# Attention scores from 32-row strips of TensorE, queries unpadded, on one core

## The reference, cut to what matters

```
x = x + conv51x51(groupnorm(x))                   # depthwise
t = tokens(x)
t = t + attn1(ln(t))   # masked: local | every 16th | first 4 keys, and a key counts only if its spike flag is set
t = t + ffn(ln(t))     # up to 33 steps; each may attend (no mask), then apply a hidden layer of 128
# attention of a sample b:  softmax(Q K^T / sqrt(32)) V, 256 x 256 scores, 32 wide
# spike flag of a key: a sequential leaky sum over the 256 tokens has crossed 1.0 in some sample
```

## Time and profile before

| what | value |
|---|---|
| median of 3 runs | 198.55 us (194.80, 198.55, 198.94) |
| profiled execution, its own time | 194.72 us |
| its span, first to last instruction | 192.6 us |
| mean granted TensorE clock | 0.965 of full |
| busy: PE, DVE, ACT, POOL | 163.9, 134.2, 106.5, 63.5 us |
| static attention from its first row maximum | 58.5 us on |
| loop attentions | about 105.7 to 138 and 146.5 to 179 us |

### The profile page before, as it was taken

One profiled execution on the slowest core, in us unless ns is written; L12 is line 12 of the kernel. 1 busy time (PEld: TensorE's weight loads), 2 busy tenths in 40 slices (PEclk: granted clock), 3 DMA queues, 4 the chain that ended last, 5 costly groups with the idle time before them and its releaser, 6 DMA issues.

```text
span 192.6 us, 4240 instructions
## 1 busy us (share of the span) xinstructions
PE 163.9 (85%) x1255; PEld 111.2 (58%) x1256; DVE 134.2 (70%) x382; ACT 106.5 (55%) x319; POOL 63.5 (33%) x153
## 2 busy tenths in 40 slices
PE   7999997773898998888966899998676999997970
PEld 5779754331684765656523687775334977673420
DVE  1363668839948889896554789789475897987371
ACT  3464511429768656565552687665375685664350
POOL 8850000100073455453600036555300075546000
PEclk9999999997599999999999999999999999999696
DMA  5900000000000000000001000000000000000003
GB/s 146 334 12 0 3 0 3 0 3 2 0 2 0 2 0 3 0 0 19 2 0 21 0 0 2 3 0 0 3 17 0 0 0 0 0 0 0 0 0 114
DMA packets 3020, 3.33 MB, mean 17 GB/s; under 512 B 889, under 2 KB 2361, under 8 KB 3002
## 3 DMA queue, kind: packets, MB, share of 16 engines
q1 hardware_dynamic: 2858, 2.85, 4.8%
q10 hardware_dynamic: 144, 0.25, 0.4%
HBM read 2.58 MB, written 0.53 MB: 16 GB/s over the span
## 4 chain that ended last, share of the span: by engine, by line
PE 61%; DVE 16%; ACT 8%; issue 7%; POOL 2%; DMA 2%; DVEq 1%; SPq 1%; POOLq 0%; ACTq 0%
PE bank L555 17%; PE bank L528 8%; PE bank L615 6%; PE bank L542 5%; ACT qz L989 4%; PE bank L798 3%; PE bank L679 3%; PE bank L512 3%; DVE big L1285 3%; PE bank L633 3%; PE bank L600 2%; POOL prob L448 2%; DMA wa<-wa_dram 2%; ACT prob L913 1%; ACT qz L1093 1%
## 5 line engine op out<-in xcount | busy, mean ns | idle before, releaser
L448 POOL TENSOR_SCALAR prob<-prob,einv 128x256 f32<-128x256 f32 x96 | 44.7, 478 | 58.9 <-DVE einv L1280 58.7
L1285 DVE COPY big<-bank 128x512 f32<-128x512 f32 x48 | 32.9, 685 | 5.8 <-PE bank L528 5.7
L913 ACT ACTIVATE prob<-bank,nmax 128x256 f32<-128x256 f32 x64 | 29.8, 474 | 11.6 <-DVE nmax L1272 11.6
L528 PE MATMUL bank<-ident,prob 128*128 128x128 f32 x192 | 30.2, 280 | 6.5 <-POOL prob L448 6.4
L555 PE MATMUL bank<-hT,qz 128*128 128x256 f32 x128 | 32.7, 383 | 0.0
L528 PEld LDWEIGHTS bank<-ident,prob 128*128 128x128 f32 x192 | 21.4, 140 | 18.2 <-POOL prob L448 14.1
L1272 DVE TENSOR_REDUCE nmax<-bank 128x2 f32<-128x512 f32 x32 | 21.6, 686 | 4.8 <-PE bank L555 4.6
L555 PEld LDWEIGHTS bank<-hT,qz 128*128 128x128 f32 x128 | 22.3, 190 | 3.6 <-issue 1.6
L913 ACT ACTIVATE prob<-minus,nmax 128x256 f32<-128x256 f32 x32 | 16.0, 500 | 8.9 <-DVE nmax L1269 7.9
L555 PE MATMUL bank<-kt,qz 128*128 128x256 f32 x64 | 16.6, 387 | 0.9 <-ACT prob L913 0.9
L913 ACT ACTIVATION_READ_ACCUMULATOR prob<-bank,nmax 128x1 f32 x64 | 13.0, 203 | 0.0
(11 more groups left out here) (172 smaller groups left out, 246.3 us busy)
## 6 DMA issues: line engine op xcount, KB each, us to landing
xrev<-xrev_dram SPq DMA_DIRECT2D x1, 512.0 KB, 4.6
xin<-xtok_dram SPq DMA_DIRECT2D x1, 512.0 KB, 5.6
out_dram<-outT SPq DMA_DIRECT2D x2, 256.0 KB, 3.3
maskc<-maskc_dram SPq DMA_DIRECT2D x1, 256.0 KB, 5.5
kx<-kx_dram ACTq DMA_DIRECT2D x1, 248.0 KB, 3.1
wx<-wx_dram SPq DMA_DIRECT2D x1, 216.0 KB, 3.6
constf<-constf_dram SPq DMA_DIRECT2D x1, 186.0 KB, 4.7
wa<-wa_dram SPq DMA_DIRECT2D x3, 56.0 KB, 1.8
```

The source lines that it names most:

```text
L448: last = nc.gpsimd.tensor_scalar(prob[b % NPB][:, ih, :], prob[b % NPB][:, ih, :], einv[:, b, ih:ih + 1], 1.0, ALU.mult, ALU.mult)
L528: mm = pe.transpose(bank[2 + b % 2][:, jh * S + ih * P:jh * S + (ih + 1) * P], prob[b % NPB][:, ih, jh * P:(jh + 1) * P], ident)
L913: e = nc.scalar.activation(prob[b % NPB][:, ih, :], scores, ACT.Exp, bias=nmax[:, b, ih:ih + 1], scale=-1.0 if masked else 1.0, accum_out= ...
L1285: nc.vector.tensor_copy(flat(probT[b % NTB]), bank[2 + b % 2][:, :]).then_inc(s_PT, 1)
```

## The change

- qz becomes qT (128, 4, 256), unpadded, and the fill of qz with zeros goes.
- `scores` takes a list of samples. Each product uses only the sample's 32 rows of queries and keys, at the row strip 32 q of TensorE (`tile_position=(q * C, 0)`), and the strips are issued next to each other: first four samples, then two at a time, after `turn_pe(b)` of an even b and ahead of `weigh_pe`. There are four score banks, SCORES = (0, 1, 4, 5), and a fourth `minus` buffer.
- Reuse of a score bank waits in the masked attention for the row maximum, no longer for the exponentials.
- The ring of tasks has two banks. Query, key and value projections work on two groups at once: half as many tasks, of 512 columns, each drained by one copy of 128 x 512.
- DVE stays three samples ahead with its row maxima.
- The filler products between the first masked scores and the first turn are 20 ahead of the spike wait and 10 behind the transposes, instead of 6 behind them; 5 more follow in both kernels.

```
-        RING = 3
-        SCORES = (0, 1, 4)
+        RING = 2
+        SCORES = (0, 1, 4, 5)
...
-        PRE = "A" + "A" + "AD" + "A" + "AAAA" + "AAAA" + "AAAA" + "D" + "AA"
+        PRE = "A" + "A" + "AD" + "A" + "AA" + "AA" + "AA" + "D" + "AA"
-        LPRE = "ADAD" + "ADAD"
+        LPRE = "AD" + "AD"
...
-            nc.gpsimd.memset(qz[:, :, :], 0.0).then_inc(s_zero, 1)
...
-            def scores(b):
-                if b >= AHEAD:
-                    wait(pe, s_P, base, b - AHEAD + 1)
-                if not masked and b % GB == 0:
-                    t.drained(pe, b // GB + 1)
-                for ih in range(NH):
-                    mm = pe.matmul(bank[SCORES[b % AHEAD]][:, ih * S:(ih + 1) * S], qz[:, b, ih * P:(ih + 1) * P],
-                                   keys[:, b // GB, :], start=True, stop=True)
-                mm.then_inc(s_S, 1)
-            for b in range(AHEAD):
-                scores(b)
+            def scores(batches):
+                last = batches[-1]
+                if last >= AHEAD:
+                    wait(pe, s_nm if masked else s_P, base, last - AHEAD + 1)
+                if not masked and batches[0] % (2 * GB) == 0:
+                    t.drained(pe, batches[0] // (2 * GB) + 1)
+                for ih in range(NH):
+                    for b in batches:
+                        g, q = divmod(b, GB)
+                        rows = slice(q * C, (q + 1) * C)
+                        mm = pe.matmul(bank[SCORES[b % AHEAD]][:, ih * S:(ih + 1) * S], qT[rows, g, ih * P:(ih + 1) * P],
+                                       keys[rows, g, :], start=True, stop=True, tile_position=(q * C, 0))
+                        if ih == NH - 1:
+                            mm.then_inc(s_S, 1)
+            scores(range(AHEAD))
             if meanwhile:
                 meanwhile()
             if masked:
+                masked(bank[2], 20)
                 pe.wait_ge(s_spk, 1)
                 product_pe(pe, st, K_CNT, onesb[:, :], spk[:, :], S)
                 for h in range(NH):
                     transposed_pe(pe, K_RES + h, tok, h)
-                masked(bank[2], 6)
+                masked(bank[2], 10)
             for b in range(MAIN):
-                if b + AHEAD < B:
-                    scores(b + AHEAD)
                 if masked and b == 0:
                     masked(bank[2], 5)
                 turn_pe(pe, base, b)
+                if b % 2 == 0 and b + AHEAD < B:
+                    scores(range(b + AHEAD, b + AHEAD + 2))
...
-                    for g in range(0, NG, 2):
-                        t.filled(act, g)
-                        for q in range(GB):
-                            rows = slice(q * C, (q + 1) * C)
-                            cp = nc.scalar.activation(qz[rows, g * GB + q, :], t.bank(g)[rows, 0:S], ACT.Copy)
-                        cp.then_inc(s_da, 1)
+                    t.filled(act, 0)
+                    nc.scalar.activation(flat(qT[:, 0:2, :]), t.bank(0)[:, :], ACT.Copy).then_inc(s_da, 1)
...
-                for b in range(AHEAD):
+                for b in range(AHEAD - 1):
                     row_max(base, b, masked)
...
-                    if b + AHEAD < B:
-                        row_max(base, b + AHEAD, masked)
+                    if b + AHEAD - 1 < B:
+                        row_max(base, b + AHEAD - 1, masked)
```

More of the change, by code:

```diff
@@ L466, in _ @@
             for g in range(NG):
-                wait(pool, s_da, 0, count("A", STATIC[:K_V + g + 1]))
+                wait(pool, s_da, 0, count("A", STATIC[:K_V + g // 2 + 1]))
                 for h in range(NH):
@@ L674, in _, with values @@
             to_tokens(3)
-            def values(t, k, src, g, w):
+            def values(t, k, src, i, w):
                 t.fill_wait(pe, k)
                 for h in range(NH):
-                    mm = pe.matmul(t.bank(k)[:, h * P:(h + 1) * P], src[:, g, h * P:(h + 1) * P], w, start=True, stop=True)
+                    for g in (2 * i, 2 * i + 1):
+                        at = (2 * h + g % 2) * P
+                        mm = pe.matmul(t.bank(k)[:, at:at + P], src[:, g, h * P:(h + 1) * P], w, start=True, stop=True)
                 mm.then_inc(s_task, 1)
@@ L915, in attention_act @@
                 e.then_inc(s_P, 1)
[L916 to L917 removed]
+                if meanwhile and b == 0:
+                    meanwhile()
                 if not masked and b >= 6 and (b - 6) % GB == 0:
```

83 lines of the change are left out of this document (37 added, 46 removed).

## The result

The changed kernel took 199.59 us (median of four executions, 198.95 to 201.56), the kernel before on the same chip 196.68 us (194.3 to 198.94). The ratio is 1.0255, with a 95% interval of 1.0213 to 1.0297: slower by 2.6%, where 1.6% faster was forecast.

What follows compares the result with a forecast made beforehand. PE was taken as the bound (busy 19.50 of 20.00 us), DVE close behind (17.66). Loops 2.4 + static 1.3 - clock 0.45 = 3.2 us gained: 198.55 - 3.2 = 195.3 us, -1.6%; range for 8 in 10, 190.5 to 198.8.

Steps and rivals of the forecast that it cites:

- The clock: Static front: PE idle 3.0 us before the spikes may drop to 1.2 GHz; cost 0 to 0.9, taken as 0.45 us.
- the last way to be wrong: Closing sign against the forecast: clock low in one of the attentions themselves, where PE has more idle time; no size given.
- Rival 2: Static front: clock stays at 1.2 GHz through all 15 fillers, turn 0 comes 3 us late; total 197.6 us; chance 20%.
- Rivals 1 and 3: 1: DVE's rate bounds, groups 5.4, 188.9 us, 15%; 3: strips don't overlap or shape changes cost more, 205 us, 10%.
- Rival 4: Attention start: the first scores at once could still wait for the second projection bank; left at nothing.
- The pair of scores: PE in the attentions: two samples in row strips take 1.00 us instead of 1.74; same for the first four.
- The loop attention's steady part: Loop groups of four samples stay at about 6.7 us, DVE's copy stalling 1.1 behind scores and weigh; no gain.
- the 0.2 that they were to give back: Loop attentions: small weight copies (four of 0.22, one of 0.18) fall into DVE's stall, returning 0.2 us.
- The forecast's sum for before: Loop attention before the change: PE's own work for four samples, shape changes included, put at 6.5 to 6.6 us.
- The loop attention's start: Each loop attention: merged projections, fewer query copies and four samples' scores at once bring turn 0 1.2 us earlier.
- The static attention: Earlier count and first row maximum (57.4), shorter periods (7.15 per four samples): 1.3 us gained at full clock.
- The wait for `K_RES + 1`: Static attention: second half of `tok` waits for K_CNT's drain, ACT's copy runs 58.25 to 58.9, taking back most of 1.1 us.

Runs made afterwards that it cites:

- fill_all: Changed kernel plus POOL's value bias after the spikes, 32 spare products ahead of them, two before turns, eight behind each loop attention's values: 190.16 us, ratio 0.9796; repeat 190.41.
- bias_late: Changed kernel, but POOL adds the value bias only after the spikes are ready: 203.35 us (198.07 to 205.84).
- front_held: Changed kernel with POOL's bias after the spikes and 32 instead of 20 spare products ahead of them, none added in the loops: 199.43 us.
- weigh_later: fill_all with the weigh of groups 0 and 1 and following copies one turn later, one spare product instead of two, at other samples: 185.03 us, ratio 0.9491.
- before_weigh_later: Kernel before the change with only the weigh of groups 0 and 1 and the copies behind it one sample later: 195.96 us against 194.95.
- padded_pairs: Changed kernel's order, but scores multiply all 128 rows of padded queries, one product after the other: 210.85 us, ratio 1.081.
- old_order: Kernel before with unpadded queries, 32-row scores and projections for two groups at once, but its queue order and one sample at a time: 225.19 us.
- fill_rows32_b: Second run of fill_all with the spare products inside the attentions on 32 rows instead of 128: seven executions, 187.97 to 206.54 us, ratio 0.9677.

## Why the prediction was wrong

**The step that failed is "The clock".** It looked for low clock in the static front alone and took 0.45 us, 0 to 0.9. There the price was far more: the 15 spare products, at 0.50 for most of their 5.12 us, ended with turn 0 at 64.40, where 61.5 was forecast and fill_all has 61.09. Between bias_late and front_held, which differ in 12 spare products ahead of the spikes and so in the clock of this stretch, the last static copy moves from 89.85 to 87.61: 2.2 us for a term of 0.45. But the larger part lay where the step had nothing, in the loop attentions: 6.1 and 2.6 us against before, and 5.8 and 2.3 against fill_all. Together the changed kernel, 199.59, stands some 9 us above the same change at a held clock (190.2 to 190.4, POOL's later bias included; by the ratios 4.6 to 5.5%). The forecast had named this as the last way to be wrong ("the clock is low in one of the attentions themselves, where PE now has more idle time than before") and given it neither a case nor a chance. The evidence was in the rows that it read: the earlier trace rows showed a fall after a stretch with PE busy a third of the time, and its own arithmetic took the scores ahead of the first turn from 2.79 us to 1.00 while POOL stayed where it was. By its own times the values end at 110.7 and turn 0 follows at 112.75: a pause of 2 us, at full clock, which it didn't cost. What the runs showed in place of the 0.45: some 2.2 us in the static front and some 8 in the loop attentions (5.8 and 2.3), where the clock was at 0.50 for 23.9 us.

**Rival 2** had the right mechanism, and in the static front its place too (15 spare products in 5.12 us where it had 6.4, turn 0 2.9 us late where it had 3); but it ended at 197.6, since it looked at that front alone. Rivals 1 and 3 didn't come: groups are not 5.4 us, and strips overlap. Rival 4 neither.

**The pair of scores**, 1.00 us of PE, measured 1.06; four at once 1.08 (108.58 to 109.66). Right to within a tenth.

**The loop attention's steady part**, "about 6.7 us" in four samples: 6.74 for a group at full clock. The mechanism held too (the copy idles 0.90 behind scores and weigh, ACT's group copy 2.20 behind the weigh), and weigh_later takes most of it away. The other group, 7.33, is that of before (7.34); small copies of DVE lie in it, and the 0.2 that they were to give back didn't come. The forecast's sum for before, 4 x (0.87 + 0.43) + 1.00 and 0.2 to 0.3, makes 6.4 to 6.5, not its 6.5 to 6.6; measured were 6.59.

**The loop attention's start**, 1.2 us: from the first weight product to the first inversion 5.69 us (106.67 to 112.36), before 6.95, so 1.26, and 1.27 in the second.

**The static attention**, 1.3 us at full clock. The wait for `K_RES + 1` is there (58.53, idle 0.33 behind the mark), but the copy into outT came at 59.69, not 58.25, and the first exponentials at 60.27, not 58.95: the collision below and the low clock. The period of 7.15 measured 7.27, 7.37 before. The first row maximum was to come at 57.4 and came at 58.39: the collision of POOL's bias with DVE's sweeps, about 1.0 us, was missed. The values, and with them POOL's eight additions, came ahead because PE was free, and in the trace of before they start at 53.58, behind the last scan (51.85 to 52.53). With it removed and the clock held, fill_all's first inversion is 0.93 us ahead of before and its last copy 1.3 us, which is the forecast's sum, though only with an edit that the forecast didn't have.

**The sum at a held clock.** 3.2 us with 0.45 for the clock, so 3.65 without. In the table fill_all is 6.4 us ahead of before. The terms of the forecast make 3.0 of them: 1.3 the static attention, 0.9 and 0.8 the loops (1.2 at the start of each, less 0.3 to 0.4 in its groups). The rest has other places: 2.5 at the end of the kernel, where the clock of before was low from 179.3 to 182.7 and that of fill_all was not (before_weigh_later, at full clock there, takes 11.6 us for it where before took 13.4 and fill_all 10.9: 1.8 for the clock, 0.7 unexplained), and 0.9 between the static attention and the first loop, where the loop's weights (`wa`) were on PE 4.95 us after their index before (99.64 to 104.59) and 3.88 in after. PE waits there for their transfer, which is issued 1.8 us behind the index in both and used 3.1 us later in before, 2.0 in after and 2.1 in fill_all; over all runs it is 2.0 to 3.2, in kernels with this loop entry alike, so this part is chance as far as the profiles show. By medians fill_all is 5.2 and 5.3 us ahead.

**What stays open.** How much of the fall is pause and how much is rows. Neither alone fits all that was seen. The profiles together show this of the start of the loop attentions. With 32-row scores and the pause of 1.98 us ahead of the first turn, the clock fell within 2.2 us of that turn in 8 of 12; with 128-row scores and the same pause (padded_pairs) in none of 2. With 32-row scores and the pause filled up to 0.14 to 0.26 us it fell in 1 of 12, and that one was filled with 32 rows. In the four profiles with 128-row scores the clock never fell between an attention's first turn and its last copy; of the thirteen with 32-row scores it did in nine, and the four others had spare products all through the attentions. So the rows go with the falls, and pauses make them likelier. But 32 rows don't force the clock down: old_order ran its static attention at 1.00 and came back to 1.00 inside its second loop attention, and spare products of 32 rows held it in 7 of 11. All 32-row products here also sit on a strip, so that the array changes its shape between them and the turns; whether the rows or that change does it wasn't tried, nor how two strips side by side count against one. Why executions of one kernel on one chip differ (188.0 and 206.5 for fill_rows32_b) the profile doesn't show.

## What to carry to other kernels

When a change takes work from TensorE, go through its timeline for the pauses that the missing work leaves, above all at the start of a phase, and price every stretch behind them at either level of the clock; the row of granted clock comes before the busy times in reading the result. In these runs, products on a quarter of the array's rows bought time in the queue and cost more of it in the clock, so try the change once with spare full-height products in its holes before judging it (here 199.6, and 190.2 us with them and POOL's later bias). And engines that were kept apart by a late producer may meet: look at what each earlier result starts on POOL beside DVE.

## What the runs showed of the hardware that was not expected

- 40.6 us of uninterrupted PE work at a granted clock of 0.50 (old_order), 33.9 us (fill_rows32_b), with 32-row products between the turns; the same order with 128-row products at 1.00. The fall in fill_rows32_b came behind a stretch with PE busy 3.25 of 3.40 us.
- Behind the same pause of 1.98 us on PE, ahead of the first turn of a loop attention, the clock fell within 2.2 us in 8 of 12 profiled loop attentions with 32-row scores and in none of 2 with 128-row scores.
- Products on different row strips ran side by side although all those of one strip were issued first: 1.14 us for eight, in either order.
- A scan of 16 partitions on DVE took 0.82 us beside POOL's additions and 0.68 alone, its scaling 0.37 and 0.28; POOL's eight additions took 4.69 us beside the scans and 3.39 behind them, in before.
- Executions of one kernel on one chip took 187.97 to 206.54 us, with mean clocks of 0.998 to 0.898.
